# An embedding tower on one core: GpSimd waits for the landing of each four gathers in the first chunk as well

## The chip, the cores and the metric

One core of one Trainium2 chip runs the whole program. The metric is the device time of one execution in microseconds, and times of the kernel before are compared with times of the kernel after on the same chip.

## The reference

For each of 2048 samples, 40 ids pick one row of 64 floats each out of 40 tables. Every pair (i, j) of the 40 fields has its own 64 x 64 matrix, and the pair's number is a bilinear form of the two rows. The 780 numbers and 16 dense features then go through three layers (512, 256, 1).

```python
e = jnp.stack([tbl_0[ids[:, 0]], ..., tbl_39[ids[:, 39]]], axis=1)      # (2048, 40, 64)
p, q = e[:, rowidx], e[:, colidx]                                       # all 780 pairs
z = jnp.einsum('bie,fie,bif->bi', p, param, q)
h = jnp.concatenate([z, dense_ctx], axis=1)
h = jnp.maximum(h @ W_top1 + b_top1, 0.0)
h = jnp.maximum(h @ W_top2 + b_top2, 0.0)
y = h @ W_top3
```

## The kernel before

The batch is cut into four chunks of 512 samples (c = 0 to 3). The 40 fields are held in pairs: a tile m (0 to 19) has fields 2m and 2m+1. GpSimd fetches a tile with eight indirect DMAs (L402), which the text calls gathers: for each of the two fields (f) four blocks of 128 samples (t), each gather taking 128 rows of 256 bytes. They go in the order of the tiles, 160 gathers to a chunk, and each adds 16 to the semaphore `gathered[slot]` of its buffer. Tiles 0 to 3 of a chunk have buffers of their own, in two sets that the chunks use in turn; tiles 4 to 19 share six buffers, so GpSimd may have to wait until TensorE has transposed the tile that was in the buffer before (semaphore `transposed`).

TensorE waits for all of a tile's gathers (L579), transposes the tile (L582, four 128 x 128 blocks) and ScalarE copies it to `e_t` (L418). The work of a chunk is then 200 items of two products each. A unit (L607) multiplies pair matrices by a tile, and a wide item (L612) does four of the first tiles' matrices at once for one block of samples. VectorE multiplies each product by the other field's rows (L522 and L519 for units, L535 for wides). TensorE sums the products of the units over the features with a matrix of ones (L630, in groups of some 16), and ScalarE (L457), in the first chunk in part VectorE (L546), sums those of the wides.

All engines follow one list of items written out in advance, row m after row m in the first chunk. A row has few items at the start and many at the end: row m begins at item 0 (m = 1), 8 (m = 4), 18, 24, 32, 40 (m = 6 to 9), 50, 60, 72, 84 (m = 10 to 13) and 180 (m = 19). TensorE's own stream is in that order too: the transpose of tile m stands just ahead of an item that `prep_at` names: 8, 10, 16, 22, 30, 38, 40, 49, 60, 71, 84 for m = 4 to 14 and 161 for m = 19; tiles 20 to 23, which are the first of chunk 1, stand at items 177, 186, 186 and 199. TensorE blocks there until the tile has landed. The products go through a ring of seven PSUM banks, so TensorE can be about three items ahead of VectorE. The layers of chunk c are worked in among the items of chunk c+1.

SyncE loads the pair matrices in pieces of twelve columns, and, once, behind the first transpose, 2.3 MB for the layers.

Of the kernel before, what the change touches and what calls it, by code (L numbers as in the profile page):

```python
# [157 lines left out]
def through(n):  # L158

    return 2 * (n + 1)  # L160
# [66 lines left out]
def slot_of(tile):  # L227


    c, m = divmod(tile, TILES)  # L230
    if m < FIXED:
        return fixed_slot(c) + m, c // 2 + 1
    n = c * (TILES - FIXED) + m - FIXED
    return 2 * FIXED + n % G_SLOTS, n // G_SLOTS + 1
# [53 lines left out]
def bilinear_tower(nc, tables, idx, dense_t, weights, w1z, b1c, w2p, b2c, w3c, out):  # L288
    with ExitStack() as ctx:
# [62 lines left out]
        @block.sync  # L352
        def _(sp):
            def load(piece):
                slot = piece % W_SLOTS
                start, n, _ = PIECES[piece]
                sp.dma_start(w[:, slot, :n * P], weights[:, start * P:(start + n) * P]).then_inc(w_in[slot], 16)

            def load_idx(c):
                sp.dma_start(idx_now[:, c % 2, :], idx[:, c * IDX:c * IDX + IDX]).then_inc(idx_in, 16)  # L360

            load_idx(0)
            load(0)

            sp.wait_ge(transposed, 1)
            load_idx(1)
            for piece in range(1, W_SLOTS):
                load(piece)
            for dst, src in ((b1[:, :], b1c), (b2[:, :], b2c), (w3[:, :], w3c), (w2[:, :, :], w2p), (w1[:, :], w1z)):
                sp.dma_start(dst, src).then_inc(mlp_in, 16)  # L370
            for piece in range(W_SLOTS, len(PIECES)):

                sp.wait_ge(t_ready, through(PIECES[piece - W_SLOTS][2]))
                load(piece)
                for c in range(2, CHUNKS):
                    if piece == IDX_BEHIND[c]:

                        sp.wait_ge(transposed, (c - 1) * TILES)
                        load_idx(c)

        @block.gpsimd
        def _(pool):
            nc.gpsimd.memset(ident[:, :], 0.0).then_inc(consts, 1)
            pool.wait_ge(consts, 1)
            nc.gpsimd.affine_select(out=ident[:, :], in_=ident[:, :], compare_op=ALU.not_equal, fill=1.0,
                                    base=0, pattern=[[-1, P]], channel_multiplier=1).then_inc(consts, 1)
            pool.wait_ge(idx_in, 16)
            for tile in range(ALL_TILES):
                c, m = divmod(tile, TILES)
                slot, use = slot_of(tile)  # L390
                if c > 0 and m == 0:
                    pool.wait_ge(idx_in, 16 * (c + 1))
                if m < FIXED and use > 1:

                    pool.wait_ge(t_free, through(PLACE[c - 2, "wide", NW - 1]))
                elif use > 1:

                    pool.wait_ge(transposed, max(t for t in range(tile) if slot_of(t)[0] == slot) + 1)
                for f in range(2):
                    for t in range(BT):  # L400
                        col = (m * 2 + f) * BT + t
                        nc.gpsimd.indirect_dma_start(  # L402
                            out=rows[:, slot, t, E * f:E * f + E], out_offset=None, in_=tables[m * 2 + f],
                            in_offset=bass.IndirectOffsetOnAxis(ap=idx_now[:, c % 2, col:col + 1], axis=0),
                        ).then_inc(gathered[slot], 16)
                    if c > 0:

                        pool.wait_ge(gathered[slot], 16 * BT * (f + 1 + 2 * (use - 1)))

        @block.scalar  # L410
        def _(act):
# [64 lines left out]
            for n in range(ALL_ITEMS + max(GROUP_LAG) + 1):  # L476
                for tile in TILES_AT.get(n, ()):
                    prepare(tile)
                if n == NI:
                    act.wait_ge(mlp_in, 5 * 16)  # L480
                if n in STEPS_AT:
                    finish_step(*STEPS_AT[n])
                if n in TURNS_AT and n < ALL_ITEMS:
                    copy_half(TURNS_AT[n])
                for c, t in Z_ORDER:
                    if t < ZS and group_at(c * GROUPS + Z_FIRST[t + 1] - 1) == n:
                        copy_z(c, t)
                done = n - REDUCE_LAG
                if 0 <= done < ALL_ITEMS and ITEMS[done][1] == "wide":
                    c, _, v = ITEMS[done]  # L490
                    if not reduced_by_vector(c, v):
                        reduce(c, v)
# [283 lines left out]
```

## Time and profile before

| | before |
|---|---|
| median of 3 runs | 1405.21 us |
| lowest and highest run | 1401.72 and 1406.98 us |
| the profiled execution | 1401.97 us |
| its span in the trace | 1400.2 us |
| TensorE busy in the span | 1260.3 us, 90% |
| VectorE, ScalarE, GpSimd busy | 71%, 74%, 43% |

The profiled execution is 1.8 us longer than its span, and 3.2 us shorter than the median of the runs. In the rows PE is TensorE, DVE is VectorE, ACT is ScalarE and POOL is GpSimd. A wait in brackets is the idle time ahead of an instruction with what ended it; where it says "remote" or "another core or an unknown queue", the profile found no event that it could name as the releaser.

### The profile page before, as it was taken

What the parts mean: (1) busy time and instruction counts of PE and PEld (TensorE: products, weight loads), DVE (VectorE), ACT (ScalarE), POOL (GpSimd) and SP (SyncE); (2) the same over time, 40 slices, a digit from 0 to 9 for tenths busy, and PEclk for the clock granted to TensorE, in tenths of its full rate; (3) what the DMA queues carried; (4) which work ended last, traced back from release to release, by engine and by line L of the source; (5) the groups of instructions that cost most, each with busy time, mean ns of one, the idle gap of its engine ahead of it and who ended that gap; (6) DMA issues with size and microseconds to landing.
All of it is one profiled execution on the core that took longest, in us unless ns stands there. A gap on an engine that the chain in (4) does not pass through costs nothing.

```text
span 1400.2 us, 23412 instructions
## 1 busy us (share of the span) xinstructions
PE 1260.3 (90%) x5952; PEld 535.6 (38%) x5952; DVE 990.6 (71%) x1615; ACT 1029.3 (74%) x7945; POOL 606.1 (43%) x646
## 2 busy tenths in 40 slices
PE   1124879699999999999999999999999999999999
PEld 0002333244444444444344444444343444444343
DVE  0104777478988778778888778777888778688880
ACT  0003668486864889889995889889996799899981
POOL 7774553655322555555523555555414565000000
PEclk9756788799999999999999999999999999999999
DMA  4111121222221222222212222122211222111100
GB/s 163 26 26 39 45 65 40 57 53 64 60 67 53 56 56 66 65 65 65 66 46 58 66 68 65 43 66 66 75 48 44 66 67 65 47 46 47 40 2 0
DMA packets 31840, 77.78 MB, mean 56 GB/s; under 512 B 11924, under 2 KB 12436, under 8 KB 31576
## 3 DMA queue, kind: packets, MB, share of 16 engines
q1 hardware_dynamic: 11088, 55.12, 12.2%
q0 software_dynamic: 20480, 21.01, 7.4%
q8 instruction: 47, 0.77, 0.2%
q14 instruction: 89, 0.73, 0.2%
q10 hardware_dynamic: 136, 0.14, 0.1%
HBM read 76.22 MB, written 0.01 MB: 54 GB/s over the span
## 4 chain that ended last, share of the span: by engine, by line
PE 78%; ACT 9%; another core or an unknown queue 8%; issue 5%; DVE 1%; ACTq 0%; DVEq 0%
PE ring L607 34%; PE z_ps L630 16%; PE ring L612 15%; ACT wide_prod L457 8%; PE ring L636 7%; PE ring L582 3%; PE ring L640 1%; ACT e_t L418 1%; DVE prod L522 1%; PE ring L643 1%; DVE wide_prod L535 0%; PE ring L589 0%; ACT z_t L430 0%; ACT L418 0%
## 5 line engine op out<-in xcount | busy, mean ns | idle before, releaser
L457 ACT ACTIVATE wide_prod<-wide_prod 128x64 f32<-128x64 f32 x3904 | 934.0, 242 | 62.9 <-issue 36.3
L402 POOL DMA_INDIRECT rows<-tbl,idx_now x640 | 605.4, 946 | 582.6 <-DMA rows<-tbl,idx_now 215.1
L522 DVE TENSOR_TENSOR prod<-ring,e_t 128x512 f32<-128x512 f32 x1008 | 628.8, 682 | 262.4 <-PE ring L607 103.6
L457 ACT ACTIVATION_READ_ACCUMULATOR wide_prod<-wide_prod 128x1 f32 x3904 | 738.3, 189 | 37.6 <-issue 36.9
L607 PE MATMUL ring<-e_t,w 64*128 64x512 f32 x2176 | 615.3, 623 | 63.8 <-issue 39.4
L535 DVE TENSOR_TENSOR wide_prod<-ring,rows 128x512 f32<-128x512 f32 x512 | 328.1, 682 | 101.9 <-PE ring L612 74.9
L607 PEld LDWEIGHTS ring<-e_t,w 64*128 64x128 f32 x2176 | 260.5, 191 | 342.6 <-issue 210.1
L612 PE MATMUL ring<-w,e_t 64*128 64x512 f32 x1024 | 321.7, 633 | 40.7 <-DVE prod L519 24.7
L630 PE MATMUL z_ps<-prod,strip 128*32 128x512 f32 x2096 | 253.1, 595 | 0.2
L612 PEld LDWEIGHTS ring<-w,e_t 64*128 64x128 f32 x1024 | 119.7, 192 | 172.0 <-issue 81.3
L418 ACT ACTIVATE e_t<-ring 128x512 f32<-128x512 f32 x80 | 45.8, 587 | 168.7 <-remote 87.8
L630 PEld LDWEIGHTS z_ps<-prod,strip 128*32 128x32 f32 x2096 | 65.3, 109 | 178.6 <-issue 150.2
L636 PE MATMUL ring<-z_t,w 128*128 128x512 f32 x224 | 99.5, 597 | 0.0
L582 PE MATMUL ring<-ident,rows 128*128 128x128 f32 x320 | 52.5, 295 | 33.0 <-DMA rows<-tbl,idx_now 28.2
L582 PEld LDWEIGHTS ring<-ident,rows 128*128 128x128 f32 x320 | 35.5, 146 | 87.1 <-issue 71.3
L636 PEld LDWEIGHTS ring<-z_t,w 128*128 128x128 f32 x224 | 41.4, 190 | 54.5 <-issue 48.4
L519 DVE TENSOR_TENSOR prod<-ring,e_t 64x512 f32<-64x512 f32 x80 | 54.8, 685 | 7.9 <-issue 3.6
L430 ACT ACTIVATE z_t<-z_ps 128x512 f32<-128x512 f32 x20 | 11.8, 590 | 43.2 <-PE z_ps L630 42.4
L466 ACT ACTIVATE h<-ring,b 128x512 f32<-128x512 f32 x16 | 11.0, 685 | 42.6 <-PE ring L636 40.2
L640 PE MATMUL ring<-h,w 128*128 128x512 f32 x64 | 28.9, 597 | 0.0
L640 PEld LDWEIGHTS ring<-h,w 128*128 128x128 f32 x64 | 11.7, 190 | 14.7 <-issue 12.4
L546 DVE TENSOR_REDUCE z_b<-wide_prod 128x16 f32<-128x1024 f32 x12 | 14.5, 1211 | 0.1
(17 smaller groups left out, 31.9 us busy)
## 6 DMA issues: line engine op xcount, KB each, us to landing
w<-weights SPq DMA_DIRECT2D x64, 768.0 KB
rows<-tbl,idx_now POOLq DMA_INDIRECT x640
w<-weights SPq DMA_DIRECT2D x4, 512.0 KB
w<-w1z SPq DMA_DIRECT2D x1, 1792.0 KB
w<-w2p SPq DMA_DIRECT2D x1, 512.0 KB
idx_now<-idx SPq DMA_DIRECT2D x4, 80.0 KB
z_t<-dense_t ACTq DMA_DIRECT2D x8, 16.0 KB
y_out_dram<-h ACTq DMA_DIRECT2D x4, 2.0 KB
```

The lines of the kernel that those rows point to most:

```text
L402: nc.gpsimd.indirect_dma_start(out=rows[:, slot, t, E * f:E * f + E], out_offset=None, in_=tables[m * 2 + f], in_offset=bass.IndirectOffse ...
L418: nc.scalar.activation(e_t[:, m, :], ring[:, BANKS["tile", tile][0], :], ACT.Copy).then_inc(e_ready, 1)
L457: last = nc.scalar.activation(products, products, ACT.Copy, accum_out=z_b[:, h, t, col:col + 1])
L519: nc.vector.tensor_tensor(dst[half, 0, :], ring[half, bank, :], e_t[half, m - 1 + j, :], ALU.mult).then_inc(t_free, 1)
L522: nc.vector.tensor_tensor(dst[:, j, :], ring[:, bank, :], e_t[:, k, :], ALU.mult).then_inc(t_free, 1)
L535: nc.vector.tensor_tensor(dst[:, j, :, :], src[:, bank, :, :], rows[:, fixed_slot(c):fixed_slot(c) + FIXED, t, :], ALU.mult).then_inc(t_fr ...
L582: last = nc.tensor.transpose(dst[:, P * t:P * t + P], rows[:, slot, t, :], ident[:, :])
L607: nc.tensor.matmul(dst, w[field, slot, P * o:P * o + P], e_t[field, m - 1 if diagonal and b == 0 else m, :], start=True, stop=True).then_i ...
L612: nc.tensor.matmul(dst, e_t[field, m, P * t:P * t + P], w[field, slot, P * o:P * o + FIXED * P], start=True, stop=True).then_inc(t_ready, 1)
L630: last = nc.tensor.matmul(z_ps[32 * col:32 * col + 32, :], strip[:, 30 - 2 * r:62 - 2 * r], prod[:, (c * NU + u) % PROD_SLOTS, jj, :], sta ...
L636: return nc.tensor.matmul(dst, w1[:, t * H1 + P * h:t * H1 + P * h + P], z_t[:, Z_NUMBER[c, t] % Z_SLOTS, :], start=start, stop=stop)
L640: return nc.tensor.matmul(dst, w2[:, k, P * h:P * h + P], h1[:, k, :], start=k == 0, stop=k == KH1 - 1)
```

## The change

In the first chunk GpSimd issued all gathers without a wait for their landing; from the second chunk on it waits behind each four until these four have landed. The new condition makes it wait in the first chunk too, behind every four but the very first (m = 0, f = 0). Nothing else differs.

```diff
                         ).then_inc(gathered[slot], 16)
-                    if c > 0:
+                    if c > 0 or m > 0 or f > 0:
 
                         pool.wait_ge(gathered[slot], 16 * BT * (f + 1 + 2 * (use - 1)))
```

## Rows read from the trace of the kernel before

**Rows 1.** The page: the span in 40 slices of 35 us, tenths busy, granted clock.

```profile
PE   1124879699999999999999999999999999999999
PEclk9756788799999999999999999999999999999999
```

**Rows 2.** Stretches of the span: length, busy time and count per engine, clock, DMA.

```profile
0.00:186.00 186.00, 77.19 (x269) 32.59 (x270) 61.13 (x92) 48.63 (x328) 119.08 (x131) 0.76 0.22 61
186.00:245.00 59.00, 47.53 (x184) 20.47 (x186) 42.72 (x67) 42.61 (x325) 28.37 (x30) 0.86 0.18 46
245.00:266.00 21.00, 8.33 (x49) 2.39 (x47) 2.11 (x4) 6.01 (x38) 13.56 (x15) 0.74 0.20 56
266.00:321.00 55.00, 55.00 (x262) 25.07 (x264) 45.72 (x76) 42.33 (x328) 30.88 (x34) 0.94 0.24 64
321.00:444.00 123.00, 122.67 (x645) 52.76 (x643) 106.85 (x177) 84.89 (x664) 37.18 (x40) 1.00 0.20 55
444.00:752.00 308.00, 305.94 (x1493) 129.80 (x1491) 244.28 (x401) 269.38 (x2101) 151.58 (x161) 1.00 0.22 61
```

**Rows 3.** The chain that ended last, from 30 to 120 us: start, length, what.

```profile
44.18 32.97 another core or an unknown queue
...
77.77 36.55 another core or an unknown queue
```

**Rows 4.** Timeline of TensorE, first 50 us: start, length, instruction, idle before.

```profile
14.37 1.09 PE L582 MATMUL ring<-ident,rows 128*128 128x128 f32 x4 [14.37 <-DMA rows<-tbl,idx_now]
29.26 1.11 PE L582 MATMUL ring<-ident,rows 128*128 128x128 f32 x4 [13.80 <-DMA rows<-tbl,idx_now]
...
47.53 0.66 PE L582 MATMUL ring<-ident,rows 128*128 128x128 f32 x4
```

**Rows 5.** Timeline of ScalarE: the copy of tile 3.

```profile
77.17 0.60 ACT L418 ACTIVATE e_t<-ring 128x512 f32<-128x512 f32 x1 [32.99 <-remote]
```

**Rows 6.** Timeline of VectorE in the first 120 us.

```profile
93.97 0.69 DVE L522 TENSOR_TENSOR prod<-ring,e_t 128x512 f32<-128x512 f32 x1 [4.91 <-remote]
...
112.17 0.68 DVE L519 TENSOR_TENSOR prod<-ring,e_t 64x512 f32<-64x512 f32 x1 [1.41 <-remote]
```

**Rows 7.** Timeline of GpSimd: gathers 8, 16, 80 and 81, then 161, 165, 169.

```profile
11.84 0.95 POOL L402 DMA_INDIRECT rows<-tbl,idx_now  x1 [0.30 <-issue]
...
21.85 0.95 POOL L402 DMA_INDIRECT rows<-tbl,idx_now  x1 [0.30 <-issue]
...
101.90 0.95 POOL L402 DMA_INDIRECT rows<-tbl,idx_now  x1 [0.30 <-issue]
114.57 0.95 POOL L402 DMA_INDIRECT rows<-tbl,idx_now  x1 [11.72 <-remote]
...
251.56 0.94 POOL L402 DMA_INDIRECT rows<-tbl,idx_now  x1 [0.30 <-issue]
...
257.97 0.94 POOL L402 DMA_INDIRECT rows<-tbl,idx_now  x1 [1.72 <-DMA rows<-tbl,idx_now]
...
264.42 0.95 POOL L402 DMA_INDIRECT rows<-tbl,idx_now  x1 [1.75 <-DMA rows<-tbl,idx_now]
```

**Rows 8.** Timeline of VectorE, 240 to 270 us.

```profile
265.18 2.48 DVE L522 TENSOR_TENSOR prod<-ring,e_t 128x512 f32<-128x512 f32 x4 [18.76 <-remote]
```

**Rows 9.** VectorE's waits, 0 to 320 us: total us, times, longest.

```profile
DVE prod L522 <- remote: 70.2, 10, 18.8
```

**Rows 10.** VectorE's two largest waits from 320 us to the end.

```profile
DVE prod L522 <- PE ring L607: 82.7, 40, 4.4
DVE wide_prod L535 <- PE ring L612: 64.8, 21, 5.1
```

**Rows 11.** GpSimd's waits for landings from 251.5 us to the end.

```profile
POOL rows L402 <- DMA rows<-tbl,idx_now: 215.1, 109, 3.9
```

**Rows 12.** Timeline of TensorE, 180 to 245 us: the transpose of tile 10.

```profile
185.88 0.66 PE L582 MATMUL ring<-ident,rows 128*128 128x128 f32 x4
```

## The prediction

> **What bounds the kernel now.** I read the page by slices first. TensorE is at nine tenths from the ninth slice to the end, and the eight slices before it, 280 us, hold nearly all of its idle time; its clock is low in the same slices [rows 1]. Stretches of the span say how far the work is at each point, because every item is two products on VectorE. The four chunks are alike in items, yet the second takes 308 us and has the first chunk's layers in it, while the first ends at 444 us [rows 2]. From 321 to 444 us it runs 177 VectorE operations, 88.5 items, in 123 us: 1.39 us an item with TensorE never idle. At that pace 200 items are 278 us; 444 - 278 = 166 us of the first chunk are start and loss.
>
> Next, the chain of waits over the start: two pieces of 33.0 and 36.6 us have no releaser with a name [rows 3]. So I set the engines' timelines side by side. TensorE transposed tile 3 from 47.53 us, 0.66 us long [rows 4]. ScalarE, which has nothing else to do then and waits for that transpose alone, copies the tile at 77.17 us [rows 5]. That is 29 us between the work and the moment the next engine sees it. VectorE shows the same in small steps: its operations of row 3 come 0.69 + 4.91 = 5.60 us apart, and 0.68 + 1.41 = 2.1 us apart at 112 us [rows 6]. GpSimd issues gathers without a break every 1.25 us until 102 us and then stops for 11.7 us [rows 7]; the steps shorten once it has stopped. A second such hole has VectorE idle 18.8 us up to 265.18 us [rows 8], in the longest unbroken run of gathers after the first: twelve, from 251.56 less eight gathers or 241.5 us on, and then waits with gaps of 1.7 us from 257.97 us [rows 7]. Waits for a nameless releaser cost VectorE's unit products 70.2 us in the first 320 us [rows 9]; after 320 us, where gathers go in fours for most of the time, no wait of VectorE for TensorE is over 5.1 us [rows 10].
>
> My reading: while gathers are issued without a pause, TensorE's completion signals reach the other engines late and one by one; where GpSimd pauses for each landing, they come at once. The first chunk is not bound by the arrival of rows: tile 10's eight gathers are issued from 114.57 us on, by 8 x 1.25 us later or 124.6 us, and its transpose comes at 185.88 us [rows 7, 12].
>
> **The change, part by part.** It adds 39 waits (40 fours less the first), and no instruction that works.
>
> What a wait costs GpSimd: two of the waits of the second chunk show gaps of 1.72 and 1.75 us where an unbroken pair has 0.30 us [rows 7], so 1.42 us more; the mean of all 109 is 215.1/109 = 1.97 us, 1.67 us more, because some meet the loads of pair matrices [rows 11]. The first chunk loads these too, so I take 1.67 and keep 1.42 as the low end. A tile then takes 8 x 1.25 + 2 x 1.67 = 13.3 us (12.8 at the low end). 39 x 1.67 = 65 us would be the whole price if GpSimd set the end.
>
> The Trainium skill (DMA: Bandwidth & Descriptors, Anatomy of one DMA — SWDGE (gpsimd) path) gives a gather a fixed 2.0 us or so, most of it the write receipt at the end. By that figure as the added gap a tile would be 14.0 us, and tile 11 would be 8 us later: some 1346 us in the end instead of my figure. The trace's gap decides.
>
> When tiles land now: tile 0 is untouched but for the wait behind it, and was transposed 1.6 us after its last gather ended (12.79, 14.37 us). Tile 1's transpose came 6.5 us after its last (22.8, 29.26 us) [rows 4, 7], 4.9 us more, in the stretch where SyncE loads the layers' weights. Unbroken issue runs over that delay, a wait doesn't: it shifts all later tiles once, 5 us (10 if both of a tile's waits meet it). So tile m lands at 14.3 + 5 + 13.3 m: 125.7 (m = 8), 152.3 (10), 165.6 (11), 178.9 (12), 192.2 (13), 272 us (19).
>
> TensorE must have tile m at its `prep_at`; transpose and copy take 2 us, and the items from there to 200 take 1.39 us each [rows 2]. The end of the first chunk is the latest of these:
>
> m = 8: 125.7 + 2 + 170 x 1.39 = 364;
> m = 10: 152.3 + 2 + 160 x 1.39 = 377;
> m = 11: 165.6 + 2 + 151 x 1.39 = 378;
> m = 12: 178.9 + 2 + 140 x 1.39 = 376;
> m = 13: 192.2 + 2 + 129 x 1.39 = 374;
> m = 19: 272 + 2 + 39 x 1.39 = 328.
>
> So rows arrive in time from tile 12 on, and up to tile 11 the gathers set the pace. TensorE idles there and its clock will be low at about 150 us, as it is in the slow slices now (0.76 up to 186 us, 0.86 behind it [rows 1, 2]). I add 2 us for its climb: 380 us. Bounds: with 12.8 us a tile m = 13 would give 368 us; if the 44 items from 40 to 84 keep the pace that they have now in the stretch from 186 to 245 us (67 operations, 1.77 us an item [rows 2]), 154 + 78 + 116 x 1.39 = 393, and 398 with another 5 us from the loads.
>
> Behind the waiting GpSimd stand only its own gathers, and for those the transposes. Tile 10 needs the buffer of tile 4, transposed at about 75 us and asked for at 139: the 11.7 us stop goes. Tiles 20 to 23 would land by 325 us at the latest and are wanted from item 177 on, 380 - 23 x 1.39 = 348 us: 23 us of cover. If that were gone, each missing us would be one. From the second chunk on nothing changes, because there the waits already stand.
>
> The sum: 444 - 380 = 64 us less. The profiled execution was 1401.97 us: 1401.97 - 64 = 1338 us. The median of the runs is 3 us above the profiled one; I leave that in the range.
>
> **The rivals.**
>
> Late signals fade but stay (chance 0.15). In favour: the 18.8 us hole outlasted the first gap at 256 to 258 us and ended at 265.18, after the second [rows 7, 8]. Against: [rows 10]. Price: one step of 4.9 us for each of the tiles 10 to 16, 7 x 4.9 = 34 us: 1372 us.
>
> No change (chance 0.06). The lateness belongs to the start of a program and not to the gathers; rows then still arrive in time, since tile 10 lands at 152 and is transposed at 186 us [rows 12]: about 1402 to 1405 us. For it: the worst steps are all in the first 115 us. Against it: the hole at 246 to 265 us. The same section of the Trainium skill says that many descriptors can be emitted before their cost shows, and puts a semaphore update at about 100 ns; by that, gathers could not hold up a signal, and it is this rival. The 29 us of tile 3 speak against that.
>
> Slower (chance 0.08). A signal of TensorE is passed on once in so many gathers: 5.60 us is 4.5 gathers at 1.25. With waits four gathers take 6.67 us instead of 5.0, so each step becomes 7.5 us. The steps fill 44 to 114 us, 70 us: a third more is 23 us: 1425 us. It decides from the point where waits leave the count per signal unchanged; that signals are prompt from 320 us on, with as many gathers per us as the waits allow, is against it [rows 10].
>
> **How the numbers follow.** My forecast, with the lateness gone, has 0.71: 1338 us, its own range 444 - 368 and 444 - 398 off: 1326 to 1356. The range for 8 in 10 takes in half of the first rival and a little at the fast end, for items without group sums that may run under 1.39 us: 1320 to 1373. A measurement of this kernel tells apart about 0.5%, 7 us. Faster: 0.71 + 0.15 = 0.86; within 0.5%: 0.06; slower: 0.08.
>
> **What would show it.** In the trace after: GpSimd's first-chunk gathers in fours with gaps of about 1.7 us; ScalarE's copy of tile 3 at about 61 us, within 2 us of its transpose; the steps of 5.6 us gone; TensorE waiting for gathers up to tile 11 or so, tile 10's transpose at about 152 us; the 18.8 us hole gone; the first chunk's last item at about 380 us and from there 956 us to the end of the span, as now. Wrong if nameless waits of VectorE remain in the first 200 us, or if tile 10 lands after 165 us.

## The result, and the profile after

On the chip of the first measurement the kernel after took 1351.8, 1352.7 and 1357.7 us and the kernel before 1399.9 to 1407.0 us in four runs; the ratio is 0.965, with an interval from 0.960 to 0.969. A fourth run of the kernel after took 2470.3 us, is counted as a slow one and left out of the ratio. The profiled execution took 1352.7 us, its span is 1350.9 us. The forecast was 1338 us, with a range of 1320 to 1373. That is one chip. Later in the study the same two kernels met on another chip, where before took 1282.7 us and after 1329.3 us: there the change makes the kernel 3.4% slower. Both results are told below, and the second matters as much as the first.

The page of the kernel after, in 40 slices of 34 us, shows TensorE at seven tenths or more from the fourth slice on. Before it was the ninth [rows 1].

```profile
PE   0458799999999999999999999999999999999999
PEclk9868799999998999999999999999999999999999
```

In stretches cut as in [rows 2] (length; busy time and count of PE, PEld, DVE, ACT, POOL; clock; DMA), VectorE has done 418 operations at 384 us. Before, it had done 416 at 444 us.

```profile
0.00:186.00 186.00, 106.85 (x407) 44.69 (x409) 87.80 (x136) 74.97 (x559) 102.97 (x114) 0.85 0.23 67
186.00:245.00 59.00, 59.00 (x285) 25.96 (x281) 50.22 (x83) 47.34 (x372) 31.39 (x34) 1.00 0.22 60
245.00:266.00 21.00, 21.00 (x102) 9.29 (x100) 19.17 (x33) 17.22 (x139) 11.80 (x13) 1.00 0.23 59
266.00:321.00 55.00, 54.60 (x289) 22.71 (x288) 45.67 (x75) 41.78 (x332) 32.48 (x35) 1.00 0.24 65
321.00:384.00 63.00, 62.76 (x331) 27.24 (x331) 54.84 (x91) 37.39 (x282) 34.99 (x38) 1.00 0.26 68
384.00:698.00 314.00, 309.29 (x1490) 131.32 (x1488) 243.76 (x401) 269.14 (x2098) 166.69 (x177) 0.99 0.23 62
```

ScalarE's timeline answers to [rows 5]. The copy of tile 3 names the transpose as its releaser, and it comes at 57.76 us instead of 77.17.

```profile
57.76 0.60 ACT L418 ACTIVATE e_t<-ring 128x512 f32<-128x512 f32 x1 [12.33 <-PE ring L582]
```

VectorE's largest waits from 0 to 320 us answer to [rows 9]. The 70.2 us for a nameless releaser are gone; what is left has TensorE's name on it and is the arrival of rows.

```profile
DVE prod L522 <- PE ring L607: 65.9, 12, 33.7
DVE wide_prod L535 <- PE ring L612: 36.7, 8, 10.1
```

TensorE's transposes of tiles 10 and 11 answer to [rows 12]. Both wait for their gathers; tile 10 comes at 150.13 us and not at 185.88.

```profile
150.13 1.11 PE L582 MATMUL ring<-ident,rows 128*128 128x128 f32 x4 [4.79 <-DMA rows<-tbl,idx_now]
164.87 1.09 PE L582 MATMUL ring<-ident,rows 128*128 128x128 f32 x4 [3.22 <-DMA rows<-tbl,idx_now]
```

A wait for gathers appears at a place where the prediction had none. In TensorE's timeline from 408 us on, tile 30 (tile 10 of the second chunk) waits 2.35 us, and the group of sums behind it takes 5.97 us. The same 34 instructions in the kernel before, at 480.86 us, take 4.48. The difference is the clock: in the kernel after the granted clock is 0.50 from 421 to 424.7 us, right behind the stall, and 0.74 from there to 430.7; in the kernel before it is 1.00 over the whole group.

```profile
421.67 1.11 PE L582 MATMUL ring<-ident,rows 128*128 128x128 f32 x4 [2.35 <-DMA rows<-tbl,idx_now]
...
424.72 5.97 PE L630 MATMUL z_ps<-prod,strip 128*32 128x512 f32 x34
```

### The profile page after: what moved, and what is told of

It is laid out like the page before. It is cut to its first block, busy times and chain, and to the rows that moved or that the text cites. A ratio compares the mean times of both kernels' runs of the same rounds, so it can differ in the third digit from the quotient of the medians.

```text
span 1350.9 us, 23423 instructions
## 1 busy us (share of the span) xinstructions
PE 1260.9 (93%) x5952; PEld 533.5 (39%) x5952; DVE 989.5 (73%) x1615; ACT 1024.3 (76%) x7945; POOL 606.2 (45%) x646
## 4 chain that ended last, share of the span: by engine, by line
PE 63%; POOL 14%; issue 9%; DMA 9%; ACT 3%; DVE 2%; another core or an unknown queue 0%; ACTq 0%; POOLq 0%; DVEq 0%
PE ring L607 26%; POOL rows L402 14%; PE z_ps L630 13%; PE ring L612 12%; DMA rows<-tbl,idx_now 8%; PE ring L636 7%; ACT wide_prod L457 2%; PE ring L640 2%; PE ring L582 2%; DVE prod L522 1%; DVE wide_prod L535 1%; PE ring L643 1%; PE ring L589 0%; ACT e_t L418 0%
## 5 line engine op out<-in xcount | busy, mean ns | idle before, releaser
L457 ACT ACTIVATE wide_prod<-wide_prod 128x64 f32<-128x64 f32 x3904 | 933.4, 242 | 41.3 <-DVE wide_prod L535 22.8
L457 ACT ACTIVATION_READ_ACCUMULATOR wide_prod<-wide_prod 128x1 f32 x3904 | 737.3, 189 | 21.1 <-issue 20.5
L607 PEld LDWEIGHTS ring<-e_t,w 64*128 64x128 f32 x2176 | 257.1, 189 | 285.9 <-issue 177.0
```

Of the source, the lines that this page charges most:

```text
L457: last = nc.scalar.activation(products, products, ACT.Copy, accum_out=z_b[:, h, t, col:col + 1])
L607: nc.tensor.matmul(dst, w[field, slot, P * o:P * o + P], e_t[field, m - 1 if diagonal and b == 0 else m, :], start=True, stop=True).then_i ...
```

## The experiments

Each kernel was measured beside the kernel before on its own chip, and chips differ. So each time is given with that of before. The edits are against the kernel after. The first four kernels share a chip (before 1390.7 us, the median of twelve runs), the next four another (1397.1 us, one run). The kernels of experiments 2 to 8 and 11 were timed once each, so small differences between them count for little; their traces count for more. The experiments ran on five chips, and the record does not say whether the chip of the first measurement is one of these.

In experiments 3, 5 and 6 the cuts leave out the new semaphore `filled`, its counter `fills`, and one wait of ScalarE in the second chunk for the last fill.

**1. A wait behind each eight gathers.**

```diff
-                    if c > 0 or m > 0 or f > 0:
+                    if c > 0 or f > 0:
```

> In the first chunk GpSimd waits behind each eight gathers (a whole tile) and not behind each four. Theory A (late signals need a long unbroken run of gathers, and a pause every eight still clears them): a tile takes 10.0 + 1.7 = 11.7 us instead of 13.3, the first chunk ends at about 360 instead of 384 us, tile 30 no longer makes TensorE wait in the second chunk (6 us): 1351 - 24 - 6 = 1321 to 1330 us. Theory B (every gather beyond the fourth in a run holds signals back): steps of about 5 us come back between the pauses, and the time lies between 1355 and 1400 us.

1385.1 us against 1390.7, ratio 0.994 (0.992 to 0.996). Theory A fails and B holds. GpSimd does go faster, but signals are late again behind tile 6, and the waits for a nameless releaser are back: VectorE's from 0 to 320 us show 26.3 us for wides alone.

```profile
DVE wide_prod L535 <- remote: 26.3, 6, 16.5
```

Copies of tiles 0 to 5 were all on time (tile 5's transpose at 75.39 us, its copy at 76.54), a point that experiment 9 uses.

**2. A wait that never pauses.**

```diff
+                    elif m > 0 and f == 0:
+                        last_slot, last_use = slot_of(tile - 1)
+                        pool.wait_ge(gathered[last_slot], 16 * BT * 2 * last_use)
```

(with `if c > 0:` for the old wait).

> In the first chunk the wait in the middle of a tile is for the tile before, which has landed by then: at most eight gathers are in flight, but GpSimd never pauses. Theory A (what clears the signals is the pause in issuing): as the kernel before, 1395 to 1410 us, with the nameless waits of VectorE back, some 70 us in the first 320. Theory C (what matters is how many gathers are outstanding): signals prompt, a tile in 10 us, 1310 to 1325 us.

1391.3 us against 1390.7, the time of before. The condition itself allows up to twelve gathers in flight, not eight. But GpSimd passes nearly every one of these waits without a stop (in the first 100 us one gap is 1.28 us, all others 0.30 or 0.31), so each tile has landed by the time four gathers of the next are issued, and at most four are outstanding there. Signals are late all the same: few outstanding gathers do not make them prompt. VectorE's waits to 320 us:

```profile
DVE prod L525 <- remote: 46.3, 7, 16.8
```

**3. A pause without a wait.**

```diff
+                    elif m > 0 or f > 0:
+                        if m > 0:
+                            pool.wait_ge(filled, 2 * m + f - 1)
+                        nc.gpsimd.memset(h2[:, :, :], 0.0).then_inc(filled, 1)
```

> In the first chunk no wait for landings; behind each four gathers GpSimd fills 1024 columns of an unused tile instead, some 1.4 us of work. Theory A (any pause in issuing clears the signals): as the kernel after, 1345 to 1365 us, no steps of 5.6 us. Rival (the wait for the landing itself matters, a filler does not): 1395 to 1410 us. In the second chunk ScalarE also waits once for the last fill, long done.

1362.3 us against 1390.7, ratio 0.980, one run. GpSimd's timeline shows the pause: from the end of one gather (35.19 + 0.94 us) to the next start is 1.13 us, where an unbroken pair has 0.30 and a wait for landing about 1.7.

```profile
35.19 0.94 POOL L403 DMA_INDIRECT rows<-tbl,idx_now  x1 [0.30 <-issue]
36.12 0.98 POOL L413 MEMSET h<- 128x1024 f32 x1
37.26 0.95 POOL L403 DMA_INDIRECT rows<-tbl,idx_now  x1 [0.17 <-issue]
```

This shorter pause, with no wait for a landing, brings more than half of the gain. Some lateness stays; the first of VectorE's nameless waits begins at 134 us:

```profile
DVE prod L528 <- remote: 27.0, 4, 10.7
DVE wide_prod L541 <- remote: 11.3, 5, 8.5
```

So a pause in issuing is enough to bring most of the gain, the landing itself needn't be awaited, and 0.8 us more than the normal gap is a little too short.

**4. No waits in any chunk.** The condition and its wait are taken out.

> The waits for landings are taken out of all four chunks, so that only buffer reuse stops GpSimd. Theory A: the first chunk as in the kernel before (ends at about 444 us), and late signals also in the later chunks wherever eight or more gathers go in a row: slower than before, 1420 to 1500 us, with nameless waits of VectorE behind 444 us. Rival (lateness belongs to the start of the program): 1400 us, later chunks unchanged.

1696.8 us against 1390.7, 22% slower, more than expected. By VectorE's counts the chunks end at 481, 894, 1305 and 1659 us, so every chunk suffers, and VectorE once stands for 49.4 us. VectorE's waits from 320 us to the end:

```profile
DVE prod L519 <- remote: 159.0, 14, 49.4
```

The lateness doesn't belong to the start of a program. It follows the gathers.

**5. Runs of sixteen at the pace of runs of four.** After experiments 1 and 3, a backlog that only grows above some mean pace (theory D) explained everything so far: eight to a wait is 0.70 gathers a us, the filler 0.69, the kernel after 0.62. This kernel holds the mean pace of after and makes the runs four times as long.

```diff
+                    elif m % 2 == 1 and f == 1:
+                        pool.wait_ge(gathered[slot], 16 * BT * 2 * use)
+                        for _ in range(4):
+                            if fills > 0:
+                                pool.wait_ge(filled, fills)
+                            nc.gpsimd.memset(h2[:, :, :], 0.0).then_inc(filled, 1)
+                            fills += 1
```

> In the first chunk GpSimd waits behind each sixteen gathers only, and then fills 1024 columns of an unused tile four times (about 4 us), so that sixteen gathers take about 25.7 us, the pace of the kernel after (12.8 us a tile), in runs four times as long. Theory D (a backlog that grows only while the mean pace is over about 0.65 gathers a us): as the kernel after, 0.96 to 0.97 of before, no signal over 3 us late. Theory B (the length of the unbroken run decides): worse than a wait behind each eight, 0.99 of before or more.

1399.3 us against 1397.1. In GpSimd's timeline sixteen gathers, a wait and the fills take 130.61 - 105.28 = 25.3 us:

```profile
105.28 3.98 POOL L416 MEMSET h<- 128x1024 f32 x4 [1.82 <-DMA rows<-tbl,idx_now]
...
130.61 3.98 POOL L416 MEMSET h<- 128x1024 f32 x4 [1.51 <-DMA rows<-tbl,idx_now]
```

The pace is right and the gain is gone. The wait behind sixteen gathers ends after 1.5 to 1.8 us, like a wait behind four: the gathers themselves don't pile up in a long run. VectorE's nameless waits to 320 us:

```profile
DVE prod L532 <- remote: 30.1, 5, 14.9
DVE wide_prod L545 <- remote: 26.5, 3, 15.5
```

Theory D falls. At one and the same mean pace runs of sixteen have late signals and runs of four have next to none, so the length of the unbroken run decides whether signals are late. It does not by itself say how late. In the kernel before, sixteen gathers go unbroken from 114.6 to 134.3 us, and VectorE's longest waits beside and just behind them are 3.67 and 5.40 us; the 18.8 us hole is beside a run of twelve. (The prediction took these twelve for the longest run after the first.)

**6. The price of the waits doubled.** The waits of after, and behind each a fill as in experiment 3.

> The waits of the kernel after, and in the first chunk a fill of about 1.1 us behind each, so a tile takes 15.5 us instead of 13.3. It doubles the price of the waits and can bring nothing more than the last few us of lateness. By the sum of the prediction the first chunk ends at 402 instead of 384 us (tiles 11 to 13 equal at 402), and in the second chunk TensorE waits for tile 30 some 20 us instead of 6: 1351 + 18 + 15 = 1384 us where before has 1402, 0.987 of before. Rival (GpSimd's pace is covered and lateness was the rest): 0.96 to 0.97.

1374.7 us against 1397.1, ratio 0.984 where 0.987 was expected. The first chunk ends at 403.4 us where the sum said 402; in the second, TensorE waits 13.5 us for gathers, where the kernel after waits 2.4 and 20 were expected. TensorE's waits in the second chunk of this kernel:

```profile
PE ring L590 <- DMA rows<-tbl,idx_now: 13.5, 2, 9.0
```

With prompt signals GpSimd's pace is the bound of the first chunk, and the formula of the prediction prices it within 2 us.

**7. Waits for tiles 0 to 9 only.**

```diff
-                    if c > 0 or m > 0 or f > 0:
+                    if c > 0 or (m > 0 or f > 0) and m < 10:
```

> In the first chunk the waits stand behind the gathers of tiles 0 to 9 only; those of tiles 10 to 19 go without, as in the kernel before. Theory D: the first 140 us as in the kernel after (tile 10 on TensorE at about 150 us), then a backlog from about 30 us later on, and a first chunk that ends between 390 and 415 us: 0.97 to 0.985 of before. Rival (only the first 115 us were harmed): 0.96 of before or better.

1408.9 us against 1397.1, one run each: 0.8% slower than before and outside what either theory expected. The first 148 us are those of after. Then the gathers run unbroken while TensorE is in full work, and it gets worse than at the start. TensorE transposes tile 10 at 148.12 us (first line, of its timeline), ScalarE copies it at 172.12 us (second line, of ScalarE's), 23 us after the transpose ended.

```profile
148.12 1.11 PE L582 MATMUL ring<-ident,rows 128*128 128x128 f32 x4 [2.81 <-DMA rows<-tbl,idx_now]
```

```profile
172.12 0.60 ACT L418 ACTIVATE e_t<-ring 128x512 f32<-128x512 f32 x1 [30.34 <-remote]
```

VectorE stands for 35.3 us and then goes in the steps of 5.5 to 5.7 us that the prediction read in [rows 6], with other products and a hundred us later:

```profile
178.51 0.69 DVE L535 TENSOR_TENSOR wide_prod<-ring,rows 128x512 f32<-128x512 f32 x1 [35.34 <-remote]
184.01 0.69 DVE L535 TENSOR_TENSOR wide_prod<-ring,rows 128x512 f32<-128x512 f32 x1 [4.81 <-remote]
189.69 0.69 DVE L522 TENSOR_TENSOR prod<-ring,e_t 128x512 f32<-128x512 f32 x1 [4.99 <-remote]
```

One part of the change alone is thus no part of the gain; the first chunk ends at 454 us here, later than before.

**8. A wait behind each eight in the second chunk.** The aim was to have tile 30 earlier.

```diff
-                    if c > 0 or m > 0 or f > 0:
+                    if f > 0 or c > 0 and not 20 <= tile < 31 or c == 0 and m > 0:
```

> As the kernel after in the first chunk; for tiles 20 to 30, the first eleven of the second chunk, the wait stands behind each eight gathers. Theory (the 6 us lost in the second chunk are TensorE waiting for tile 30, because GpSimd is the bound up to there): tile 30 lands 15 to 18 us earlier, the wait goes, 6 us less than after, 0.96 of before. Rival (the loss at item 226 has another cause, or the quicker pace makes signals late again): no gain, 0.965 or more.

1399.0 us against 1397.1. The gathers of tiles 20 to 30 are issued while TensorE still works on the first chunk, and runs of eight hold its signals back there: VectorE stands 17.9 us up to 356.71 us and 14.6 us up to 386.73, and the first chunk ends at 439 us.

```profile
356.71 3.68 DVE L522 TENSOR_TENSOR prod<-ring,e_t 128x512 f32<-128x512 f32 x6 [17.92 <-remote]
```

The question of tile 30 wasn't answered by it, but the middle of a kernel, 340 us from the start, is now shown to be exposed like the start.

**9 and 10. Eights before tile 6, and the kernel after again, on one chip.**

```diff
-                    if c > 0 or m > 0 or f > 0:
+                    if c > 0 or m >= 6 or f > 0:
```

> As the kernel after, but in the first chunk tiles 0 to 5 have one wait behind each eight gathers, and only tiles 6 to 19 one behind each four. With the wait behind each eight everywhere, no copy of tiles 0 to 5 came late, because TensorE works there just after a tile has landed, in the pause. So tiles from 6 on land about 7 us earlier with no signal late, the first chunk ends at about 377 instead of 384 us, and tile 30 comes 7 us earlier too: 7 us or 0.5% under the kernel after, 0.96 of before. Rival (lateness carries over from the runs of eight into the runs of four): no gain or a loss against the kernel after.

> The kernel after, unchanged, timed on the chip of the run above so that the two can be compared: 0.960 to 0.969 of before, as in its first measurement.

Here the kernel before took 1282.7 us, the median of eleven runs (1282.6 to 1284.3), 121 us less than at first. The kernel after took 1329.3 us, ratio 1.034 (1.032 to 1.037), and the variant 1322.2 us, ratio 1.031 (1.028 to 1.033). Both expectations failed in their ratio to before. The variant was quicker than the kernel after by 7 us, as forecast.

The kernel after is little different on this chip: its first chunk ends at 380 instead of 384 us, the third and the fourth take 300 us each instead of 311 and 305. Its stretches, chunk by chunk:

```profile
0.00:379.00 379.00, 299.85 (x1401) 128.76 (x1403) 256.94 (x414) 216.37 (x1676) 212.08 (x230) 0.91 0.23 66
379.00:690.00 311.00, 302.96 (x1491) 128.17 (x1489) 243.77 (x401) 266.69 (x2103) 166.94 (x177) 0.98 0.23 62
690.00:990.00 300.00, 299.76 (x1491) 127.30 (x1489) 243.47 (x401) 263.84 (x2082) 150.91 (x160) 1.00 0.23 63
990.00:1290.00 300.00, 299.52 (x1469) 126.61 (x1467) 243.03 (x400) 261.44 (x2077) 74.48 (x79) 1.00 0.17 49
```

No trace of the kernel before was taken on this chip, so its first chunk is worked out. Its span is 1280.9 us. Three chunks of 300 us and the last 37 us leave 344 us, a few us less if its second chunk is longer than 300. So the first chunk ends near 340 to 344 us and not at 444. The prediction's own sum says what a first chunk without waits and with prompt signals should take: with tiles landing at 19.3 + 10.0 m, m = 10 gives 119 + 2 + 160 x 1.39 = 343 us. The agreement says that on this chip the signals of the kernel before were prompt. It is an inference from times, not a row. The mean granted clock of the same runs fits it: 0.989 to 0.993 here, 0.952 to 0.974 in the runs of the kernel before on the other chips, where TensorE idles more at the start.

The two traces that were taken on this chip bear it out. On the first chip even the kernel after has 85 short gaps ahead of ScalarE's own sums (L457) for which the profile shows nothing that they wait for. This is a line of ScalarE's waits over the whole span:

```profile
ACT wide_prod L457 <- issue: 34.9, 85, 0.9
```

The kernel before has 140 of them, 73.3 us, and the kernel without waits (experiment 4) 444, 304.4 us. The same kernel after on the quick chip has none, and neither does the variant there; nor has VectorE a single nameless wait in either.

**11. No waits once more.** The edit is that of experiment 4.

> The kernel without any wait for landings once more, because the kernel before took 1282.7 us on the chip of the last two runs against 1390 to 1403 on the others. Theory E (late signals are a property of some chips, not of the program): where before takes about 1283 us, the first chunk, which has the same instructions as in before, ends at about 340 us with no copy over 3 us late, and the whole is 1283 us or less, since gathers in the later chunks only gain pace. Where before takes about 1395 us, it is near 1697 us again, with late copies. Rival (lateness comes and goes on one chip from run to run): the two times don't go together.

It met a chip of the common kind: before 1391.1 us, this kernel 1698.5 us, as in experiment 4 on another chip (1696.8). That speaks for a property of the chips and against a whim of single runs, but the kernel without waits was not measured on the quick chip.

**12. Eights before tile 6 again.** The edit is that of experiment 9.

> The kernel with eights before tile 6 once more, to have it also on a chip of the other kind. Where before takes 1390 to 1403 us (late signals): 0.957 to 0.963 of before, 0.5% under the 0.965 of the kernel after, if TensorE's work on tiles 0 to 5 falls into the pauses. Rival: lateness from the runs of eight reaches the tiles behind, 0.965 to 0.985. Where before takes 1283 us: 1.031 again.

1344.6 us against 1404.3 us, ratio 0.956 (0.953 to 0.960). The kernel after had 0.965 (0.960 to 0.969) on its chip. These two are from different chips, and the intervals only just part; on the quick chip, side by side, the variant was 7 us ahead and the intervals just met. Both comparisons point to the variant, by 0.4 to 0.9%, but neither settles it, since one sets two chips side by side and in the other the intervals meet; on the quick chip the kernel before beats both. VectorE's waits to 320 us have no nameless releaser among them; the largest is

```profile
DVE prod L522 <- PE ring L607: 60.7, 10, 32.0
```

## Why the prediction was right, and where it was off

**The reading of the first chunk** held. TensorE's completion signals were late, by 29 us for tile 3, and pausing GpSimd made them prompt, but for one (below). What the prediction couldn't tell apart, the experiments did: it is neither the number of gathers outstanding (2, 5) nor their mean pace (5) nor the time since the start (4, 8), but how many are issued without a pause (1, 5, 7). The pause need not be a wait for the landing (3).

**The price of a wait** held. Tiles 10 and 11 were forecast to land at 152.3 and 165.6 us and were transposed at 150.1 and 164.9. Tile 3's copy was forecast at 61 us and came at 57.8.

**The end of the first chunk**, 380 us in the forecast, was 384: VectorE's first product of the second chunk starts at 384.44 us where it was 444.73. The 4 us are in the pace of the items: from tile 11's transpose to the end the sum has 2 + 210 us and 2 for the clock, and it took 219.6, while the tile came 0.7 us early. Experiment 6 gave the formula a harder test, 402 forecast and 403.4 measured. One bound was added up wrongly: with 12.8 us a tile the latest of the sums is not 368 us (tile 13) but 372 (tile 11), so the fast end of the forecast's own range should have been 1330 and not 1326 us.

**The step that was mis-sized** is the sentence "From the second chunk on nothing changes", with the cover of 23 us that I worked out for tiles 20 to 23 and for no later tile. The time from there to the end of the span is 1350.9 - 384.4 = 966.5 us, where it was 1400.2 - 444.7 = 955.5: 11 us more. The second chunk has some 7 of them, and 6 of those fall between its items 220 and 230, at tile 30. Up to that tile GpSimd now never has to wait for a buffer, as it did before, where it issued tile 30 from 442 us on behind a stop of 43 us. It is one column of 31 tiles at 13.5 us that ends at 420 us, while the first chunk has moved 60 us forward. The stall itself is 2.35 us; the rest is what TensorE loses behind it at a granted clock of 0.50 and then 0.74, as the slow group of sums shows. Experiment 6 makes the waits for gathers 13.5 us and the second chunk 17 us longer than before, which shows the cause. Some 3 us more were lost in the fourth chunk. There one signal was late in spite of the waits: VectorE stands 5.38 us for a nameless releaser, up to 1124.30 us. TensorE had ended the two products that it takes next at 1117.11 us (three matmuls from 1115.99 us, 1.12 us long, of which these are the last), and the gathers around it go in fours, with gaps of 1.8 to 2.8 us.

```profile
1124.30 1.29 DVE L522 TENSOR_TENSOR prod<-ring,e_t 128x512 f32<-128x512 f32 x2 [5.38 <-remote]
```

So "prompt with a pause behind each four" is nearly but not wholly true. The working asked for 64 us and the profiled execution gained 49: 60 in the first chunk, 4 less than asked, and then 11 lost behind it.

**The rivals.** "Late signals fade but stay" is what shorter pauses or longer runs give (1, 3, 8); of the change itself it is true for 3 us and not for the 34 us of its price. "No change" fell with experiment 4. The sentence of the Trainium skill named there (DMA: Bandwidth & Descriptors, Anatomy of one DMA — SWDGE (gpsimd) path), that many descriptors can be emitted before the incremental cost shows, is about a DMA's own fixed cost, and for that the trace agrees: the gap between gathers stays 0.30 us however many go unbroken. The prediction was wrong to read from it that gathers can't hold up a signal; unbroken emission cost 306 us in experiment 4, on the other engines. "Slower" came true, on one chip, and by another mechanism than the one I gave. Where signals are prompt anyway, the waits are pure price: tiles at 13.3 instead of 10.0 us, 377 instead of 343 us for the first chunk by the same sum, and the stall at tile 30, which is 6.5 us on that chip. That is 34 + 7 = 41 us and the rest of its wake, against 46.6 us measured. The forecast had no rival for this, because one trace of one chip can't show that what it shows is the chip's.

**What stays open.** What in the chip delays the signals, and why one chip did not show it. No trace of the kernel before was taken on that chip. Nor is it known what makes one signal 29 us late and another 4, beyond the length of the run; the number of signals that TensorE sends during a run was not varied.

## What to carry to other kernels

Where an engine idles and the profile has no name for the releaser, lay the timelines of the two engines side by side: work that has ended long before its consumer starts is a late signal, and no faster engine cures it. Look then for what is issued without a pause, and break the run up; here runs of four gathers with a gap of 1.7 us were enough but for 3 us, and runs of eight were not. Before a workaround is kept, time both kernels on several chips: this one was timed on two, is worth 3.5% on one and costs 3.4% on the other.

## What the runs showed of the hardware

While GpSimd issues indirect gathers without a pause, one every 1.25 us, completion signals of TensorE reach VectorE and ScalarE late, by 29 us for tile 3, with VectorE idle for up to 49.4 us in experiment 4, and then one by one, 5.5 to 5.7 us apart. Signals in the other direction were not late where I looked: in the kernel before, TensorE starts at 77.82 us on the copy that ScalarE ended at 77.77.

```profile
77.82 5.36 PE L607 MATMUL ring<-e_t,w 64*128 64x512 f32 x14 [29.63 <-issue]
```

It isn't only TensorE's signals that suffer. The 16 sums of a wide item follow one another on ScalarE without a wait for another engine, and their instructions otherwise start 0.09 to 0.15 us apart (from 139.77 us on in experiment 7). In the late stretch of the same trace, from 176.98 us on, they start 0.70, 1.40 or 2.10 us apart. Two of them:

```profile
176.98 0.26 ACT L457 ACTIVATE wide_prod<-wide_prod 128x64 f32<-128x64 f32 x1 [1.19 <-issue]
178.38 0.20 ACT L457 ACTIVATION_READ_ACCUMULATOR wide_prod<-wide_prod 128x1 f32 x1 [1.14 <-issue]
```

VectorE's step of 5.60 us [rows 6] is eight times 0.70. No run here shows what is slowed. The ends of matmuls are modelled by the profile, so a "late signal" rests on this: behind the transpose of tile 10 in experiment 7 TensorE went on with twelve more matmuls, until 153.07 us, while ScalarE, idle all the time, began the copy only at 172.12.

The Trainium skill (DMA: Bandwidth & Descriptors, Anatomy of one DMA — SWDGE (gpsimd) path) puts the update of a semaphore behind a DMA's receipt at about 100 ns; the gathers' own waits, with gaps of 1.7 us from the end of issue, don't contradict that, but they don't show the 100 ns apart.

The lateness was there on every chip where the kernel before took between 1387 and 1411 us, and by its time not on the one where it took 1282.7. On that chip the later chunks of the kernel after are quicker too, 300 us against 305 to 311, though the gathers go in fours on both. So even with waits behind each four a few us a chunk are lost on the other chips. ScalarE's short gaps, 34.9 us there and none on the quick chip, say that the same slowing has a part in it; how large a part of the difference it makes isn't separated.
